# Half-height products side by side in an attention stage, and a third engine for the low parts

## The reference

```python
# layer 0: layer norm over channels, in_proj, 3x3 depthwise convolution, SiLU,
# a selective scan in four directions over the 4096 positions, norm, gate, out_proj, + x
x = _L0_conv_ref(x, ...)
# layer 1: non-local attention, O = 96, N = 4096
g_x, theta_x, phi_x = conv1x1(x, g), conv1x1(x, theta), conv1x1(x, phi)   # each (B, 96, 4096)
f1 = einsum('bon,bom->bnm', theta_x, phi_x)                               # (B, 4096, 4096)
y  = einsum('bnm,bom->bon', softmax(f1, axis=-1), g_x)
x  = conv1x1(y, W) + x
```

## Time and profile before

| | |
|---|---|
| median of 3 runs | 9250.66 us (9244.29 to 9259.2) |
| the profiled execution | 9256.15 us, its span 9254.4 us |
| mean granted TensorE clock | 0.981 of 2.4 GHz |
| PE, DVE, ACT, POOL busy, share of the span | 93%, 80%, 66%, 36% |
| attention of image 0, from its first score to the last product by g | 739.7 to 1192 us |

### The profile page before, as it was taken

The page is one execution under the profiler, slowest core; times in us unless marked ns, Lnnn a source line. Parts: engine busy times, 40 slices in busy tenths (PEclk is TensorE's granted clock), DMA queues, the critical chain, the costliest instruction groups (busy, mean ns, idle before and its releaser), DMA issues. The chain is left out here.

```text
span 9254.4 us, 103902 instructions
## 1 busy us (share of the span) xinstructions
PE 8642.6 (93%) x26448; PEld 4648.4 (50%) x26448; DVE 7377.0 (80%) x8229; ACT 6091.9 (66%) x7440; POOL 3295.4 (36%) x1853
## 2 busy tenths in 40 slices
PE   7899998999989998899988999889998899988999
PEld 3336743367433674336733367333673336733476
DVE  6987779877798777987679876798767987689876
ACT  6765677656776567765677556775567755677566
POOL 2870028600286002860038600385003850038400
PEclk9999999999999999999999999999999999999999
DMA  1320013200132001320013200232002320023200
GB/s 53 111 87 13 10 56 112 80 13 10 57 111 82 11 11 59 115 76 10 11 63 111 76 10 11 65 116 71 8 12 68 111 73 8 11 72 114 66 8 12
DMA packets 286693, 503.21 MB, mean 54 GB/s; under 512 B 142155, under 2 KB 143215, under 8 KB 253431
## 3 DMA queue, kind: packets, MB, share of 16 engines
q1 hardware_dynamic: 286199, 497.81, 17.9%
HBM read 467.99 MB, written 29.47 MB: 54 GB/s over the span
## 5 line engine op out<-in xcount | busy, mean ns | idle before, releaser
L1400 DVE TENSOR_TENSOR pl<-pf,ph 128x1024 fp32r<-128x1024 f32 x1024 | 1254.3, 1225 | 1007.1 <-ACT ph L1020 999.5
L1253 DVE TENSOR_TENSOR_SCAN h<-ps,h,dbu 128x512 f32<-128x512 f32 x1536 | 1884.2, 1267 | 59.8 <-POOL dbu L1087 29.9
L1087 POOL TENSOR_TENSOR dbu<-bs,du 128x1024 f32<-128x1024 f32 x768 | 1808.1, 2369 | 54.1 <-POOL du L1078 54.1
L1020 ACT ACTIVATE ph<-pf 128x1024 fp32r<-128x1024 f32 x1024 | 1085.3, 1060 | 750.3 <-PE ps L708 750.0
L885 ACT ACTIVATE ps<-dt,negA 128x512 f32<-128x512 f32 x1536 | 1037.5, 687 | 684.8 <-DVE h L1253 684.8
L1014 ACT ACTIVATE pf<-ps 128x1024 f32<-128x1024 f32 x1024 | 1050.4, 1026 | 530.7 <-PE ps L695 513.3
L1066 POOL MEMSET pad<- 128x66 f32 (+1 forms) x64 | 7.2, 200 | 3853.2 <-DVE fa L1429 3853.0
L1384 DVE TENSOR_REDUCE mx<-ps 128x1 f32<-128x512 f32 x1792 | 1168.6, 683 | 78.8 <-PE ps L606 62.5
L1261 DVE TENSOR_TENSOR hc<-h,ps 128x1024 f32<-128x1024 f32 x768 | 937.9, 1221 | 110.3 <-PE ps L487 19.7
L487 PE MATMUL ps<-xhl,selr 128*128 128x512 f32 x1536 | 768.1, 585 | 238.8 <-DVE hc L1261 238.6
L1072 POOL TENSOR_TENSOR dt<-dt,ze 128x1024 f32<-128x1024 f32 x256 | 604.0, 2359 | 1061.3 <-ACT dt L878 1061.3
(11 more groups left out here) (204 smaller groups left out, 14540.6 us busy)
## 6 DMA issues: line engine op xcount, KB each, us to landing
bs<-rows SPq DMA_DIRECT2D x256, 1024.0 KB, 5.1
bs<-rows SPq DMA_DIRECT2D x512, 256.0 KB, 6.1
xa<-in_x SPq DMA_DIRECT2D x130, 256.0 KB, 2.9
xb<-in_x SPq DMA_DIRECT2D x130, 128.0 KB, 3.0
out<-fa SPq DMA_DIRECT2D x64, 256.0 KB, 2.1
rdb<-rden SPq DMA_DIRECT2D x56, 192.0 KB, 3.4
out<-fa SPq DMA_DIRECT2D x64, 128.0 KB, 2.4
xhl<-ct SPq DMA_DIRECT2D x256, 8.0 KB
```

The lines of the kernel that those rows point to most:

```text
L1020: A(ph[:, mp % 2, :, :], pf[:, mp % 2, :, :], ACT.Copy).then_inc(S["ph_ready"], 1)
L1087: pool.tensor_tensor(dbu[:, q, :, :], bs[par][:, q, :, :], du[:, r:r + 1, :].to_broadcast([P, 2, T]), ALU.mult).then_inc(S["dbu_ready"], 1)
L1253: dve.tensor_tensor_scan(h[:, j, ::step], ps[:, 2 + e, ::step], dbu[:, q, e, ::step], h[:, j, end:end + 1], ALU.mult, ALU.add)\
L1400: TT(pl[:, mp % 2, :, :], pf[:, mp % 2, :, :], ph[:, mp % 2, :, :].bitcast(F32), ALU.subtract)\
```

## The change

- The scores of a block of 128 keys become five products of 64 rows (one of them of 33) instead of three of 97. The 3 x 96 rows and the shift's row are packed into them: `ph1`, `ph2`, `ph3` hold phi's parts, some in two places, `th1`, `thx`, `thy` theta's. A product uses either the lower 64 rows of the array or the upper 64, and the two blocks of a step stand side by side: one on the lower rows, the other on the upper (`scores_1`, six of them), then the other way round (`scores_2`, four).
- A product by g is cut into two of 64 rows, the lower halves summed in bank 4, the upper in bank 5 (`weigh`, now in two calls a step, one for each block). VectorE copies bank 5 and adds it to what ScalarE copied of bank 4 (`read_sum` in both).
- `top` is cut into a lower and an upper half, which stand at the two ends of a group of six halves; the upper one now also holds part of the low theta. Its banks are 6 and 7 instead of 5 and 6.
- `TOPS` moves the tops to steps 2 to 12; the output's parts stand at steps 13 and 15.
- GpSimd makes the low parts of `ph` in those eleven steps, VectorE in the other five.
- The shift goes in two DMAs (one for each of `thx` and `thy`) instead of four. SyncE's order is as it was.

```diff
-        TOPS = [0] + [2] * 4 + [3] * 8 + [0] * 3
+        TOPS = [0] * 2 + [2] + [3] * 10 + [0] * 3
-        DEN_AT, RB_AT, WY_AT, WR_AT = 5, 8, 10, 12
+        DEN_AT, RB_AT, WY_AT, WR_AT = 5, 8, 13, 15
+        LOW, UP = slice(0, R), slice(R, P)
+        BY_POOL = [mp for mp in range(MP) if TOPS[mp]]
+        BY_DVE = [mp for mp in range(MP) if not TOPS[mp]]
...
-                        for t in range(4):
-                            sp.dma_start(thc[1 - par][0][O:O + 1, t * P:(t + 1) * P].bitcast(F32), nmr[:, t:t + 1].bitcast(F32))\
-                                .then_inc(S["shift_loaded"], 16)
+                        for row in (thx[1 - par][LO:LO + 1, :], thy[1 - par][O:O + 1, :]):
+                            sp.dma_start(row.bitcast(F32).rearrange("o (p j) -> o p j", j=4), nmr[:, :].bitcast(F32)).then_inc(S["shift_loaded"], 16)
...
+                    if rows == LOW:
+                        if j == 0:
+                            pe.wait_ge(S["thh_ready"], i + 1)
+                            pe.wait_ge(S["thl_ready"], i * 4 + 1)
+                        pe.wait_ge(S["top_read"], i * NU + (j + 1))
+                    else:
+                        pe.wait_ge(S["top_half"], n)
+                    q = mm(ps[:, 6 + j % 2, :], th1[par][rows, :].rearrange("p (k t) -> p t k", t=4)[:, t, :], ph1[rows, m * T:(m + 1) * T],
+                           start=(rows == LOW), stop=(rows == UP))
+                    q.then_inc(S["top_half" if rows == LOW else "top_ready"], 1)
...
+                    pe.wait_ge(S["pf_ready"], s + 1)
+                    bank = 2 * (mp % 2)
+                    one, other = slice(2 * mp * P, (2 * mp + 1) * P), slice((2 * mp + 1) * P, (2 * mp + 2) * P)
+                    t1, tx = th1[par], thx[par]
+
+                    def low(n):
+                        if n < 2:
+                            return mm(ps[:, bank, :], (ph1, ph2)[n][LOW, one], t1[LOW, :], start=(n == 0), stop=False)
+                        return scores_0(mp, par, 0)
+
+                    def up(n):
+                        if n < 2:
+                            return mm(ps[:, bank + 1, :], (ph1, ph2)[n][UP, other], (t1, tx)[n][UP, :], start=(n == 0), stop=False)
+                        return scores_0(mp, par, 1)
+                    if j is not None:
+                        top(j, i + 1, c, 1 - par, LOW)
+                    for n in range(2 if mp == 0 and first else 3):
+                        if j is None:
+                            low(n)
+                            q = up(n)
+                        else:
+                            up(n)
+                            q = low(n)
+                    q.then_inc(S["s1_done"], 1)
+                    if j is not None:
+                        top(j, i + 1, c, 1 - par, UP)
+
...
+                def scores_0(mp, par, e, stop=False):
+
+                    rows = (slice(0, LO + 1), slice(R, O + 1))[e]
+                    return mm(ps[:, 2 * (mp % 2) + e, :], ph3[rows, mp * P:(mp + 1) * P], (thx, thy)[e][par][rows, :], start=False, stop=stop)
+
+                def scores_2(mp, i, par, first):
+
...
+                    mm(ps[:, bank, :], ph1[UP, one], t1[UP, :], start=False, stop=False)
+                    mm(ps[:, bank + 1, :], ph1[LOW, other], t1[LOW, :], start=False, stop=False)
+                    mm(ps[:, bank, :], ph2[UP, one], tx[UP, :], start=False, stop=not early)
+                    q = mm(ps[:, bank + 1, :], ph2[LOW, other], t1[LOW, :], start=False, stop=not early)
...
-                    for e in range(2):
-                        m = 2 * mp + e
-                        dst = ps[:, 2 * (mp % 2) + e, :]
-                        kk = phh[:, m * P:(m + 1) * P]
-                        mm(dst, kk, hi[:, :], start=not early, stop=False)
-                        q = mm(dst, phl[:, m * P:(m + 1) * P], hi[:, :], start=False, stop=early)
-                        if not early:
-                            q = mm(dst, kk, lo[:, :], start=False, stop=True)
...
-                def weigh(mp, i):
+                def weigh(mp, e, i, c, par=0, j=None):
+
...
+                    if e == 0:
+                        wait_low(pe, i, mp)
+                        if mp == 0:
+                            pe.wait_ge(S["sum4_read"], i + 1)
+                            pe.wait_ge(S["sum5_read"], i + 1)
+                    m = 2 * mp + e
+
+                    def half(n, bank, rows):
+                        g, p = ((gth, ph), (gtl, ph), (gth, pl))[n]
+                        return mm(ps[0:O + 1, bank, :], g[rows, m, :], p[rows, mp % 2, e, :],
+                                  start=(m == 0 and n == 0), stop=(m == MT - 1 and n == 2))
+                    if j is not None:
+                        top(j, i + 1, c, 1 - par, LOW)
+                    for n in range(3):
+                        if j is None:
+                            half(n, 4, LOW)
+                            q = half(n, 5, UP)
+                        else:
+                            half(n, 5, UP)
+                            q = half(n, 4, LOW)
+                    if e == 1:
...
-                        scores(mp, c, i, par, not before)
+                        blocks = list(range(FIRST_TOP[mp], FIRST_TOP[mp] + TOPS[mp])) if nxt else []
+                        third = blocks.pop(0) if len(blocks) == 3 else None
+                        blocks += [None] * (2 - len(blocks))
+                        scores_1(mp, c, i, par, not before, third)
+                        if mp >= LAG:
+                            weigh(mp - LAG, 0, i, c, par, blocks[0])
+                        elif before:
+                            weigh(mp - LAG + MP, 0, i - 1, c)
+                        scores_2(mp, i, par, not before)
...
                         if mp >= LAG:
-                            weigh(mp - LAG, i)
+                            weigh(mp - LAG, 1, i, c, par, blocks[1])
                         elif before:
-                            weigh(mp - LAG + MP, i - 1)
-                        for j in blocks[2:]:
-                            top(j, i + 1, 1 - par, j // (NU // 4), j % (NU // 4), 5 + j % 2)
+                            weigh(mp - LAG + MP, 1, i - 1, c)
...
                             if mp == WY_AT:
                                 if nxt:
                                     pe.wait_ge(S["thf_ready"], i + 2)
+                                    pe.wait_ge(S["top_read"], (i + 1) * NU + (NU + 2))
...
+                        A(ph1[O:P, bass.ds(c * T, T)], phf[R:O, :], ACT.Copy)
+                        A(ph2[O:P, bass.ds(c * T, T)], phf[LO:R, :], ACT.Copy)
+                        blocks = phf[0:LO, :].rearrange("p (a e k) -> p a e k", e=2, k=P)
+                        for e in range(2):
+                            A(ph3[e * R:e * R + LO, bass.ds(c * (2 * P), 2 * P)].rearrange("p (a k) -> p a k", k=P), blocks[:, :, e, :], ACT.Copy)\
+                                .then_inc(S["ph3_ready"], 1)
...
+                    for mp in BY_POOL:
+                        pool.wait_ge(S["ph_ready"], i * MP + (mp + 1))
+                        pool.tensor_tensor(pl[:, mp % 2, :, :], pf[:, mp % 2, :, :], ph[:, mp % 2, :, :].bitcast(F32), ALU.subtract)\
+                            .then_inc(S["plp_ready"], 1)
+                        pool.wait_ge(S["plp_ready"], i * len(BY_POOL) + (BY_POOL.index(mp) + 1))
+                        pool.sem_inc(mark, 1)
...
+                    dst = (th1[par][O:P, :], thx[par][O:P, :], thx[par][0:LO, :], thy[par][R:O, :])[n]
+                    src = slice(*((R, O), (LO, R), (0, LO), (0, LO))[n])
+                    TT(dst, thf[src, :], th1[par][src, :].bitcast(F32), ALU.subtract).then_inc(S["thl_ready"], 1)
...
+                    dve.wait_ge(S["pv_ready"], i * MP + (MP + 2))
+                    dve.tensor_copy(rdb[:, :], ps[0:O + 1, 5, :]).then_inc(S["sum5_read"], 1)
+                    dve.wait_ge(S["sum4_read"], i + 2)
+                    dve.wait_ge(S["sum5_read"], i + 2)
+                    TT(yraw[:, :], yraw[:, :], rdb[:, :], ALU.add).then_inc(S["yraw_ready"], 1)
...
+                        if mp in (1, 4, 5, 6) and nxt:
+                            low_theta(i + 1, 1 - par, (1, 4, 5, 6).index(mp))
+                        if mp == LAG and before:
+                            read_sum(i - 1)
...
+                        if mp > 0 and mp - 1 in BY_DVE:
+                            low_exp(mp - 1, i * MP + (mp - 1))
+                        for j in tops[0:]:
+                            top(j, i + 1)
+                        if nxt and mp > 0 and FIRST_TOP[mp] == NU and FIRST_TOP[mp - 1] < NU:
+                            negate(i + 1, c + 1)
...
+                    low_exp(MP - 1, i * MP + (MP - 1))
```

More of the change, by code:

```diff
@@ L138, in build @@
         thf = sb("thf", [O, T], where=vx)
-        thc = [[sb(f"thc{q}{i}", [O + 1, T], F32R, where=vx) for i in range(2)] for q in range(2)]
+        th1 = [sb(f"th1{q}", [P, T], F32R, where=vx) for q in range(2)]
```

(15 more changed lines are left out.)

128 lines of the change are left out of this document (61 added, 67 removed).

## The result

| | |
|---|---|
| changed kernel | 9787.81 us, median of 4 runs (9775.97 to 9791.03) |
| kernel before | 9251.92 us, median of 4 runs (9244.29 to 9259.2) |
| ratio | 1.0573, 95% interval 1.056 to 1.0586 |
| forecast | 9480 us, range 9130 to 9720 |

The change costs 536 us, 67 us an image. The direction was forecast; the size was not, and the time lies above the range. The two waits that were priced came nearly as priced; 305 us of the loss, more than half, came on top of the 231 of the prediction's sum.

The account below looks back on a forecast made before the run. PE was taken to bound attention, by its number of slots. The terms, -29.7 + 11.2 + 30.7 + 12 + 4 + 0.7, gave +28.9 us an image, +231 for eight: 9480 us, 2.5% slower, range 9130 to 9720.

Parts of the forecast that it names:

- 1 slots: PE in attention: halves side by side save 16 slots a chunk at 0.232 us, 29.7 us an image.
- 2 bank 4: Step 2: the first product by g waits 1.6 us for ScalarE's bank 4 read, +11.2 us an image.
- 3 shift: Ends of chunks 1 to 6: PE waits 5.1 us for the shift behind the store, +30.7 us an image.
- 4 clock: Behind each gap of 5 us PE's clock falls, 2.0 us lost each time, +12 us an image.
- 5 rest: Attention's waits for top halves, `s1_done` and bank reads: 0.5 us a chunk, +4 us an image; GpSimd keeps up.
- VectorE's add at an image's end: At the image's end VectorE's add stands ahead of the denominator: +0.7 us an image.
- ScalarE's and VectorE's additions before attention: ScalarE's extra copies before attention, 1.6 us a chunk, fit in a gap from 682.2 to 686.26: cost nothing.
- The forecast's own sign: Attention's chunk period: near 60 us in place of 56.8, and 53 to 54 without the gaps, if right.
- Pairs don't overlap: Rival, chance 0.07: PE's half products don't run at once, 1632 slots more an image, about 12,500 us.
- faster: Rival, chance 0.19: pairs run at 0.2133 us a slot and the clock holds over the gaps, 9142 us.
- GpSimd and VectorE hold each other up: Rival, chance 0.08: in steps 4 to 6 and 8 their SBUF instructions exclude each other, +110 us, 9590 us.
- No gain, no loss: Rival, chance 0.04: the shift's gap is half as long and the clock holds, about +2 us an image, 9267 us.

Follow-up runs that it names:

- the shift's repair: Changed kernel with SyncE issuing the shift's two DMAs ahead of the store of the chunk before: 9483.42 us, ratio 1.0258.
- the repaired kernel: Changed kernel with all repairs: shift first, contiguous top weights, early bank 4 read, theta work moved, VectorE in last chunk, later lower halves: 9218.6 us, ratio 0.9967.
- the run with contiguous tops: Changed kernel with the shift ahead of the store and `top` taking its weights from 128 columns side by side: 9409.88 us, ratio 1.0178.
- With the sum read early: On the run with contiguous tops, ScalarE reads bank 4's old sum ahead of its copy `ph` of step 1: 9334.11 us, ratio 1.0088.
- The kernel with full-height tops: On the kernel with all repairs, each top is one product over 96 rows and not two halves: 9810.72 us, ratio 1.0602.
- the unrolled one: On the kernel with all repairs, attention's eight chunks are written out in place of a loop over pairs: 9162.89 us, ratio 0.9898.

## Why the prediction was wrong

By its own terms, for eight images:

| term | forecast | what the runs show |
|---|---|---|
| 1 slots | -237 | pairs start together, 0.23 us apart, and steps without tops take 11 slots for 12: stands (read from the trace, not taken away by a run) |
| 2 bank 4 | +90 | waits of 98 and, for the last chunk, 11.5; repaired in part: 76, with clock |
| 3 shift | +246 | waits of 255 |
| 4 clock | +96 | about 100 behind the shift and 35 behind bank 4, where none was forecast; the shift's repair gave 304 for terms 3 and 4 together, against 342 forecast |
| 5 rest | +32 | steps with tops 0.30 us longer than 14 slots, 616 times: 185 (of it strided weights 74, a read wait 54 or more); GpSimd in the last chunk 43 by the trace, 51 repaired |
| VectorE's add at an image's end | +6 | wait of 12.7 where 5.5 stood before: 7 |
| ScalarE's and VectorE's additions before attention | 0 | 57 by the trace (7.2 us an image), 26 of it repaired |
| length of the loop | none | hidden in the changed kernel, whose list of waits has no such gap beside that for the shift; 56 in the repaired kernel |

The column on the right adds up to 555 with 43 for the last chunk, for 536 measured. The terms overlap a little, and no large one is missing.

**The mechanisms that were forecast are there.** The stall at the shift is 5.31 us for 5.1 forecast, 48 times for 48; that at bank 4 is 2.04 for 1.6, just above the upper bound given. The clock falls behind each of the first, for a loss of 2.1 us on average where 2.0 was forecast; that it would fall behind 21 of the 48 gaps at bank 4 as well was left out. A small slip lies in the range: a slot of 0.225 is worth 1632 x 0.007 x 8 = 91 us and not 100; nothing hangs on it.

**Term 5 is the step that failed**: "I take 0.5 us a chunk", 32 us in all. The runs show 3.3 us a chunk in the steps with tops (11 x 0.30) and some 5.4 in the last chunk, 230 us in all. The forecast's own sign says the same: without the gaps the period should have been 53 to 54 us; 66.1 less 5.3, 2.0 and some 2.8 for the clock is 56. The term put a lump on several things, of which two had rows or counts to be read. One, the weights of `top` with a stride of four columns, was in the diff and was not priced at all; its price (0.04 us a top) has no row in the trace of before, so it had to be bounded and not left at nothing. Two, the distance between a top and the next but one in the same bank was never counted: 8 slots, 1.86 us, against the 1.90 from the start of a top's lower half, past the end of VectorE's read, to the start of the load for the next but one (901.62 to 903.52 in the run with contiguous tops). Three, "it keeps up" was worked out for a step of 14 slots; the last chunk has 11, which is 2.55 us, and GpSimd's 2.4 with its hand-overs are 3.09 (6.17 for two steps).

**"Nothing" for the stage before attention** looked at a gap of ScalarE in a middle chunk. In chunk 0 there is no such gap: theta's split and its low parts stand there ahead of VectorE's next deviation, which PE waits for. In the changed kernel PE waits there for ScalarE's squares of that deviation (`PE ps L416 <- ACT sqb L871`, 4.3 us at the longest), and the first two steps take 7.2 us more in all, the clock's part among them.

**The slots' gain is paid back in places, none of them large.** From the kernel with all repairs, 30 us faster than the one before, to the 237 of term 1 there are 207 us. Of these 56 are the loop's (36 in attention by the trace); 56 the wait for bank 5 (`PE ps L780 <- DVE rdb L1520`, 48 times 1.2 us); 43 the steps with tops, which still take 3.32 us on average for 3.25, 616 times; about 18 what is left in the stage before. Some 34 stay without a place, or 54 with the trace's figure for the loop.

**The rivals.** "Pairs don't overlap" and "faster" fall by the starts shown above. "GpSimd and VectorE hold each other up" is right in its mechanism and wrong in its price. In the last chunk of every image VectorE's `yn`, with both operands in SBUF, starts inside one of GpSimd's low parts, here the one that runs from 1217.86 to 1220.26:

```profile
1219.35 1.46 DVE L1517 TENSOR_TENSOR yn<-yraw,rdb 96x512 f32<-96x512 f32 x1 [4.94 <-DMA rdb<-rden]
```

It takes 1.27 to 1.58 us in these eight cases, 0.68 in the others, and ends 0.55 us behind GpSimd's low part each time: it waits until GpSimd is done. The Trainium skill (SBUF — State Buffer, Who interferes with whom) has the two exclude each other for a whole instruction; the trace agrees. It costs next to nothing here, since the two seldom meet: `low_theta`, which the prediction priced for steps 4 to 6, ends 0.18 us or less after GpSimd has started, and GpSimd's low part is 0.05 us longer at most (2453 ns for 2400). VectorE's reads of tops, whose operand lies in PSUM, take 0.69 us beside GpSimd as without it. So the rival's +110 us didn't come, and the kernel before isn't slowed by GpSimd's low parts either. "No gain, no loss" falls by the gap of 5.31 us, which is not half as long, and by the clock behind it.

## What to carry to other kernels

- A wait in a queue taken in order costs by what stands behind it: ask of every queue not only what it does but whether the next thing in it is more urgent than the one that waits. Two lines in another order were worth 304 us.
- When work is cut into smaller pieces that run beside each other, count per resource (bank, load port, hand-over, loop body) the time from one use to the next in the shortest step, and in the odd chunks, first and last, by themselves. A lump "for the rest" hides exactly these.
- Once some products are in halves, make all of a step halves: a change to full height and back cost more here (0.38 us) than a product (0.23).

## What the runs showed of the hardware that was not expected

- A load of weights of 128 float32 columns takes 183 to 191 ns side by side (medians) and 306 to 309 with a step of four columns, over 64 rows as over 96. The Trainium skill (TensorE: Matmul & The Clock Gate, LDWEIGHTS) has the time go by the number of columns alone; here the number of columns is the same and the time is not.
- PE had no work for a while where the loop over pairs of chunks goes back: 2.47 us before its next load in the row shown, and 1.8 and 2.2 us longer chunks there. The changed kernel's instruction queue moves 6.00 MB in 366 packets, that of the kernel before 2.72 in 166, and the latter has no such gap in its list of waits. The kernel with full-height tops, 3.51 MB in 214, has none either, nor has the unrolled one (5.60 in 342). Which of code size and jump it is has not been taken apart.
- In the changed kernel the clock fell behind all 48 gaps of 5.3 us and behind 21 of 48 gaps of 2.0 us. With the sum read early it fell behind 2 of 54 gaps between 1.0 and 1.6 us.
- A VectorE instruction with both operands in SBUF waited for the end of GpSimd's: 1.27 to 1.59 us for 0.68, in all 16 cases of two traces (the changed kernel, and the kernel before with GpSimd's low parts).
